# Second half of v for tokens 0 to 255 moved to the third head group, x transpositions, q and k of the next block to later steps

## The chip, the core and the metric

The kernel runs on one core of a Trainium2 chip. Its engines work side by side, each through its own list of instructions: TensorE (PE: matmuls, with weight loads as PEld beside them), VectorE (DVE), ScalarE (ACT), GpSimd (POOL) and SyncE (SP, which issues the DMAs). They wait for each other through semaphores alone. The metric is the device time of one execution in microseconds (us).

## The reference

A transformer block with cross attention, in fp32, for 16 batches of 512 tokens, 512 features and 16 heads of 32, and with a hidden layer of 2048:

```python
q = _layer_norm(query, ln1_g, ln1_b)
qh = (q @ wq + bq).reshape(Bq, Sq, H, hd)
kh = (context @ wk + bk).reshape(Bq, Sc, H, hd)
vh = (context @ wv + bv).reshape(Bq, Sc, H, hd)
scores = jnp.einsum('bqhd,bkhd->bhqk', qh, kh) * scale
allowed = pos_in_block[None, :] <= jnp.arange(Sq)[:, None]
scores = jnp.where(allowed[None, None, :, :], scores, NEG_INF)
probs = jax.nn.softmax(scores, axis=-1)
o = jnp.einsum('bhqk,bkhd->bqhd', probs, vh).reshape(Bq, Sq, Dm)
x = query + o @ wo + bo
h = _layer_norm(x, ln2_g, ln2_b)
return x + jax.nn.gelu(h @ w1 + b1, approximate=False) @ w2 + b2
```

## The kernel before

Two programs follow each other in one launch. Stage A computes attention and writes x to a scratch tensor, stage B the hidden layer. The change touches stage A alone. Every dense product is made of three matmuls, since each fp32 operand is held as a high part and a low part (`_hi`, `_lo`).

Stage A runs over the 16 batches: the first unrolled, batches 1 to 14 in a hardware loop, the last and a tail unrolled. A batch is 48 steps: four head groups (`g` 0 to 3, four heads each) of twelve steps (`k` 0 to 11). Step `k` of a group brings one tile of scores through a pipeline:

- PE forms the scores in `bank_s` (L425). Steps 0 to 3 hold two matmuls (128 and 256 columns), steps 4, 6, 8 and 10 one of 384, steps 5, 7, 9 and 11 one of 512.
- DVE adds the mask and takes the minimum (L574), then moves the transposed probabilities of four steps earlier from `bank_t` to `pT` (L520). For the tiles of steps 5, 9 and 11 ACT makes this move, in its own list at steps 9, 1 and 3.
- ACT takes the exponential (L710).
- PE transposes the tile of three steps earlier into `bank_t` (L437). The tile of step `k-3` needs the bank that the tile of step `k-5` leaves, so PE waits in step `k` for the move made at step `k-1`.

Into each step PE's list puts dense work between the scores and the transpositions. Its place is written out by hand in the table `BESIDE`: for each group the jobs, and how many matmuls of a job stand in which step. The jobs are `Q0` to `Q3` and `K0` to `K3` (q and k of a head group, 12 matmuls of 512 columns; group `g` makes those of group `g+1`, and `Q0`, `K0` those of the next batch), `V0a`, `V0b`, `V1a`, `V1b` (v: 0 and 1 are tokens 0 to 255 and 256 to 511, a and b the two halves of the heads; 24 matmuls of 256 columns, L410), `X0` to `X3` (x of the next batch transposed, L369), `R` (reciprocal sums transposed, L379) and `O0` to `O3` (output product of the batch before). Outside the table, the product with v stands at step 9 for the first pair of query tiles and at step 5 of the next group for the rest (`pv`, L460).

The dense jobs take turns in three banks, `bank_d`, in the order of their first matmuls: a job waits until the job three before it has been read. Who reads is fixed: X by ACT (L676) in the step in which it ends and by DVE (L552) one step later; Q and K by ACT (L686) in the step in which they end and by DVE (L560) one step later; V by ACT (L697); R by ACT (L718). `Q0` waits for DVE's read of the last three X jobs. DVE multiplies by the reciprocals (`o_product`, L584) at step 6. When q and k of a group are split, SP copies them into `stack` with six DMAs of 256 KB (L265), in order; the group's first scores wait for all six. POOL splits the context of the next batch (L773, L775) once `V1b` is done, then expands the reciprocals that the fourth group's `R` needs. SP stores x of `O1` to `O3` and then loads x of the next batch (L336), on which DVE takes statistics at steps 1, 3, 4 and 4 of the third group (L531).

Of the kernel before, what the change touches and what calls it, by code (L numbers as in the profile page):

```python
# [51 lines left out]
def stage_a(nc, x, ctxT, wq, wk, wv, wo, vecs, bo, x1):  # L52
# [21 lines left out]

    BESIDE = [
# [4 lines left out]
    ]  # L80
    TAIL = [("R", {5: 4}), ("O0", {8: 12}), ("O1", {9: 12}), ("O2", {10: 12}), ("O3", {11: 12})]

# [23 lines left out]
    with ExitStack() as ctx:  # L106
# [246 lines left out]
        def _(pe):  # L353
# [86 lines left out]
            def pv(it, g, pair):  # L440

                last_tile = TG * g + (3 if pair == 0 else 11)
                for i in range(2):

                    pe.wait_ge(moved[i], it.b * (TB // 2) + ((last_tile + 1) // 2 + 1))
                if pair == 0:
                    pe.wait_ge(o_prod, it.b * NG + (g + 1))
                if g in (0, 2):

                    name = f"V{pair}{'ab'[g // 2]}"  # L450
                    at = {"V0a": -1, "V1a": 0, "V0b": 1, "V1b": 2}[name]
                    pe.wait_ge(d_free[it.bank(name, at)], it.bank_read(name, at))
                if pair == 0:
                    parts = [(0, 0, 256, 0), (1, 256, 128, 128)]
                else:
                    parts = [(0, 384, 256, 256), (1, 640, 256, 256), (2, 896, 256, 256), (3, 1152, 128, 256)]
                for j, at, w, to in parts:
                    for r in range(4):
                        h = 4 * (g % NG) + r
                        mm = pe.matmul(bank_v[32 * r:32 * r + 32, to:to + w], v_sb[:, j, HD * h:HD * h + HD],  # L460
                                       pT[:, r, at:at + w], start=(j == 0), stop=(j == len(parts) - 1),
                                       skip_group_check=True)
                mm.then_inc(pv_done, 1)
# [24 lines left out]
            def body(it):  # L488
                for n, steps in enumerate(it.steps):
                    g, k = divmod(n, TG)  # L490
                    if not it.tail:
                        score(it, n)
                    for job, i, j in steps:
                        dense_step(it, job, g, i, j)
                    if k == PV1_AT and not (it.first and g == 0):
                        pv(it, g - 1, 1)
                    if k == PV0_AT and not it.tail:
                        pv(it, g, 0)
                    if n >= LAG and not it.tail or n < LAG and not it.first:
                        p_transpose(it, n - LAG)  # L500
# [696 lines left out]
def build(nc, x, ctxT, wq, wk, wv, wo, vecs_a, bo, w1, w2, vecs_b, b2, out):  # L1197
    x1 = nc.dram_tensor("x1_scratch", tuple(x.shape), F32).ap()
    stage_a(nc, x, ctxT, wq, wk, wv, wo, vecs_a, bo, x1)
    stage_b(nc, x1, w1, w2, vecs_b, b2, out)  # L1200
# [41 lines left out]
```

## Time and profile before

| | |
|---|---|
| median of 3 runs | 3095.35 us (3094.23 to 3096.35) |
| the profiled execution | 3096.19 us, span 3094.5 us |
| first scores of stage A | 47.42 us |
| the 14 batches of the loop | 137.7 to 1470.8 us |
| rest of stage A (last batch, tail) | to about 1585 us |
| stage B | the remainder |
| PE busy over the span | 2965.2 us (96%) |
| DVE, ACT, POOL busy | 1520.4, 1153.1, 459.1 us |

Times in views of stretches count from the start of the span. In such a view every engine has its busy time and, in brackets, the number of its instructions; PEclk is the granted clock of TensorE as a share of 2.4 GHz. In the timeline a row holds the start, the duration, the engine, the line and the operation; in square brackets stands how long the engine had been idle before and what released it. PE's rows overlap, because matmuls are pipelined: what a matmul costs is the distance to the start of the next row. The fifth batch of the loop is quoted most: its groups begin at 519.20, 541.33, 568.62 and 591.12 us, and it ends at 614.55 us.

How long a step takes, from the first scores of one step to those of the next (starts of L425 in the timeline), in us; the fourth group is that of batch 7 (781.81 to 803.65 us), where the clock stays at 1.00:

| step | 0 | 1 | 2 | 3 | 4 | 5 | 6 | 7 | 8 | 9 | 10 | 11 |
|---|---|---|---|---|---|---|---|---|---|---|---|---|
| second group | 2.07 | 1.95 | 2.07 | 1.95 | 1.31 | 5.15 | 0.51 | 3.36 | 2.02 | 2.90 | 2.03 | 1.98 |
| third group | 2.06 | 1.95 | 2.06 | 1.95 | 1.30 | 3.79 | 1.93 | 1.00 | 1.86 | 1.94 | 2.08 | 0.56 |
| fourth group | 4.01 | 1.95 | 2.06 | 1.95 | 1.31 | 2.37 | 1.46 | 1.03 | 1.40 | 1.97 | 1.28 | 1.05 |

### The profile page before, as it was taken

The numbers are of one execution on the slowest core, as the hardware profiler recorded it, in microseconds if no ns is written. First come the engines' busy times: TensorE is split into PE (matmuls) and PEld (weight loads), VectorE is DVE, ScalarE is ACT, GpSimd is POOL, SyncE is SP. The second block draws the span as 40 slices with busy tenths as digits, with TensorE's granted clock in tenths as the row PEclk, the third lists the DMA queues.
The fourth block names the chain that finished last, engine by engine and source line by source line (L and its number), as shares of the span: only waits on it lengthen the run. The fifth ranks groups of instructions, "written<-read, shape, count | busy, mean of one in ns | idle before, by whom it ended". The sixth has DMA issues, their size and how long they took to land. (4 is left out here: it accounts for less than half of the span.)

```text
span 3094.5 us, 52560 instructions
## 1 busy us (share of the span) xinstructions
PE 2965.2 (96%) x17576; PEld 2408.6 (78%) x17576; DVE 1520.4 (49%) x4100; ACT 1153.1 (37%) x2958; POOL 459.1 (15%) x432
## 2 busy tenths in 40 slices
PE   6999999999999999999979999999999999999999
PEld 5777877778777777777758888888888888888887
DVE  4766666666676666766634333322333322333322
ACT  3655566555666565655622111111111111111111
POOL 1222122211222112222112000000000000000000
PEclk9999999999999999999979999999999999999999
DMA  5766676666666666666522111100111100111100
GB/s 133 122 113 102 111 107 111 115 110 108 107 108 119 112 102 115 103 119 110 89 85 82 41 41 41 41 9 32 41 41 41 41 31 10 41 41 41 41 27 14
DMA packets 123695, 231.89 MB, mean 75 GB/s; under 512 B 10752, under 2 KB 10752, under 8 KB 123648
## 3 DMA queue, kind: packets, MB, share of 16 engines
q1 hardware_dynamic: 123648, 231.28, 37.5%
q8 instruction: 28, 0.46, 0.1%
q14 instruction: 19, 0.16, 0.0%
HBM read 97.02 MB, written 33.55 MB: 42 GB/s over the span
## 5 line engine op out<-in xcount | busy, mean ns | idle before, releaser
L710 ACT ACTIVATE sm<-sm,mins 128x128 f32<-128x128 f32 (+3 forms) x1024 | 571.7, 559 | 606.4 <-DVE mins L574 603.6
L574 DVE CUSTOM_DVE_ANT_0 sm<-bank_s,mask 128x128 f32<-128x128 f32 (+3 forms) x1024 | 480.7, 488 | 451.2 <-PE bank_s L425 440.5
L1146 ACT ACTIVATE g_sb<-bank_f,b1s 128x512 f32<-128x512 f32 x256 | 176.2, 688 | 1173.1 <-PE bank_f L956 1173.1
L1058 DVE CAST g_hi<-g_sb 128x512 fp32r<-128x512 f32 x256 | 113.0, 441 | 866.9 <-ACT g_sb L1146 866.9
L437 PE MATMUL bank_t<-ident,sm 128*128 128x128 f32 x2560 | 424.1, 281 | 53.5 <-ACT pT L520 34.1
L437 PEld LDWEIGHTS bank_t<-ident,sm 128*128 128x128 f32 x2560 | 305.8, 143 | 156.9 <-issue 76.6
L954 PE MATMUL bank_f<-hT_hi,w_hi 128*128 128x512 f32 x1024 | 407.6, 398 | 1.6 <-DVE hT_lo L1052 1.6
L954 PE MATMUL bank_o<-w_hi,g_hi 128*128 128x512 f32 x1024 | 408.0, 398 | 0.0
L956 PE MATMUL bank_f<-hT_hi,w_lo 128*128 128x512 f32 x1024 | 406.7, 397 | 0.0
L955 PE MATMUL bank_f<-hT_lo,w_hi 128*128 128x512 f32 x1024 | 406.4, 397 | 0.0
L956 PE MATMUL bank_o<-w_hi,g_lo 128*128 128x512 f32 x1024 | 406.3, 397 | 0.0
L955 PE MATMUL bank_o<-w_lo,g_hi 128*128 128x512 f32 x1024 | 405.6, 396 | 0.0
L425 PE MATMUL bank_s<-stack 96*128 96x128 f32 (+3 forms) x1024 | 357.3, 390 | 6.5 <-DMA stack<-st_lo 5.8
L520 DVE COPY pT<-bank_t 128x384 f32<-128x384 f32 (+1 forms) x576 | 326.9, 568 | 0.5 <-PE bank_t L437 0.5
L1190 POOL TENSOR_TENSOR xr<-xr,b_row 128x512 f32<-128x512 f32 x64 | 81.3, 1301 | 1213.2 <-DMA xr<-x_scratch 1213.2
L954 PEld LDWEIGHTS bank_f<-hT_hi,w_hi 128*128 128x128 f32 x1024 | 193.4, 189 | 48.3 <-issue 2.0
L956 PEld LDWEIGHTS bank_f<-hT_hi,w_lo 128*128 128x128 f32 x1024 | 193.7, 189 | 47.4
L955 PEld LDWEIGHTS bank_f<-hT_lo,w_hi 128*128 128x128 f32 x1024 | 193.9, 189 | 46.8
L956 PEld LDWEIGHTS bank_o<-w_hi,g_lo 128*128 128x128 f32 x1024 | 193.1, 189 | 46.6
L955 PEld LDWEIGHTS bank_o<-w_lo,g_hi 128*128 128x128 f32 x1024 | 193.0, 188 | 46.2
L954 PEld LDWEIGHTS bank_o<-w_hi,g_hi 128*128 128x128 f32 x1024 | 192.8, 188 | 45.5
L792 POOL TENSOR_TENSOR oT_lo<-rT,oT_hi 128x512 fp32r<-128x512 f32 x64 | 82.3, 1286 | 814.6 <-ACT oT_hi L724 814.6
(108 smaller groups left out, 4486.5 us busy)
## 6 DMA issues: line engine op xcount, KB each, us to landing
stack<-st_hi SPq DMA_DIRECT2D x256, 256.0 KB, 5.6
xt<-in_x SPq DMA_DIRECT2D x32, 1024.0 KB, 5.3
stack<-st_lo SPq DMA_DIRECT2D x128, 256.0 KB, 7.2
c_raw<-in_ctxT SPq DMA_DIRECT2D x64, 256.0 KB, 6.0
x_scratch<-xt SPq DMA_DIRECT2D x64, 256.0 KB, 2.0
xn<-x_scratch SPq DMA_DIRECT2D x16, 1024.0 KB, 7.7
xr<-x_scratch SPq DMA_DIRECT2D x16, 1024.0 KB, 5.6
out<-xr SPq DMA_DIRECT2D x64, 256.0 KB, 2.1
```

Source lines behind the costliest of these rows:

```text
L425: mm = pe.matmul(bank_s[n % BANKS_S][:, off:off + w], stack[0:96, g % 2, 0, r, P * qt:P * qt + P], stack[0:96, g % 2, 1, r, 0:w], start=Tr ...
L437: mm = pe.transpose(bank_t[n % 2][:, P * c:P * c + P], sm[:, n % SLOTS_S, P * c:P * c + P], ident[:])
L520: copy(out, src).then_inc(moved[n % 2], 1)
L574: op = V.tensor_tensor_reduce(sm[:, n % SLOTS_S, off:off + w], bank_s[n % BANKS_S][:, off:off + w], mask[:, 512 - w:512], 1.0, 0.0, ALU.ad ...
L710: op = A.activation(row, row, ACT.Exp, bias=mins[:, g % 2, c:c + 1], scale=-1.0, accum_out=sums[:, g % 2, c:c + 1])
L792: G_.tensor_tensor(out=oT_lo[:, g % NG, :], in0=rT[:], in1=oT_hi[:, g % NG, :].bitcast(F32), op=ALU.subtract).then_inc(oT_done, 1)
L954: pe.matmul(o, lh, rh, start=first, stop=False)
L955: pe.matmul(o, lh, rl, start=False, stop=False)
L956: return pe.matmul(o, ll, rh, start=False, stop=last)
L1058: V.tensor_copy(g_hi[:, f % RING_H, :], g_sb[:, f % 2, :]).then_inc(g_hi_ok, 1)
L1146: A.activation(g_sb[:, f % 2, :], bank_f[f % 2][:], ACT.Gelu, bias=b1s[:, f:f + 1], scale=1.0).then_inc(gelu, 1)
L1190: G_.tensor_tensor(out=xr[:, t, :], in0=xr[:, t, :], in1=b2_row[:], op=ALU.add).then_inc(xr_ok, 1)
```

## The change

`V0b` leaves steps 10 and 11 of the second group for steps 4 and 5 of the third; `V1b` and the four x transpositions there go one step later; in the fourth group `Q0` goes from steps 0 and 1 to 1 and 2, `K0` from 2 and 3 to 4 and 5, `V0a` from steps 6 to 10 to steps 7 to 11. In `pv` the index under which `V0b` is looked up follows.

```diff
-        [("Q2", ...), ("K2", ...), ("R", {4: 4}), ("O1", {5: 12}), ("O2", {7: 12}), ("O3", {8: 6, 9: 6}), ("V0b", {10: 12, 11: 12})],
-        [..., ("R", {4: 4}), ("V1b", {5: 12, 6: 12}), ("X0", {7: 4}), ("X1", {8: 4}), ("X2", {9: 4}), ("X3", {10: 4})],
+        [("Q2", ...), ("K2", ...), ("R", {4: 4}), ("O1", {5: 12}), ("O2", {7: 12}), ("O3", {8: 6, 9: 6})],
+        [..., ("R", {4: 4}), ("V0b", {4: 12, 5: 12}), ("V1b", {6: 12, 7: 12}), ("X0", {8: 4}), ("X1", {9: 4}), ("X2", {10: 4}), ("X3", {11: 4})],
...
-                    at = {"V0a": -1, "V1a": 0, "V0b": 1, "V1b": 2}[name]
+                    at = {"V0a": -1, "V1a": 0, "V0b": 2, "V1b": 2}[name]
```

The number of instructions of each engine stays as it was. PE's list in the loop, from the third group's step 10 or 11 into the fourth group, right behind the four transpositions of `X3`; before:

```order
L437 MATMUL bank_t1<-ident,sm 128x128 x4
L421 REGISTER_ALU
L425 MATMUL bank_s1<-stack 128x512
L435 REGISTER_ALU
L437 MATMUL bank_t0<-ident,sm 128x128 x3
L420 REGISTER_ALU
L421 REGISTER_ALU
L425 MATMUL bank_s0<-stack 128x128
L425 MATMUL bank_s0<-stack 128x256
L390 REGISTER_ALU
L410 MATMUL bank_d2<-xnT_hi,wq_hi 128x512
```

The same place now:

```order
L435 REGISTER_ALU
L437 MATMUL bank_t0<-ident,sm 128x128 x3
L420 REGISTER_ALU
L421 REGISTER_ALU
L425 MATMUL bank_s0<-stack 128x128
L425 MATMUL bank_s0<-stack 128x256
L437 MATMUL bank_t1<-ident,sm 128x128 x4
L421 REGISTER_ALU
L425 MATMUL bank_s1<-stack 128x128
L425 MATMUL bank_s1<-stack 128x256
L390 REGISTER_ALU
L410 MATMUL bank_d2<-xnT_hi,wq_hi 128x512
```

Between `X3` and the first matmul of `Q0` there stood two sets of transpositions and two of scores; there stand as many now, but both sets of scores are those of the fourth group's steps 0 and 1, and `Q0` has moved behind step 0.

DVE's list in the fourth group in the loop, from K0's low part (`st_lo` with `vec`) to `o_product` (L584) before the change:

```order
L560 SCALAR_TENSOR_TENSOR st_lo<-bank_d,vec,st_hi 128x512
L567 REGISTER_ALU
L574 ISA sm,mins<-bank_s,mask 128x512
L574 ISA mins 128x1
L520 COPY pT<-bank_t 128x384
L567 REGISTER_ALU
L574 ISA sm,mins<-bank_s,mask 128x384
L574 ISA mins 128x1
L520 COPY pT<-bank_t 128x384
L582 REGISTER_ALU
L583 REGISTER_ALU
L584 TENSOR_TENSOR rT<-bank_v,rT 128x512
```

And DVE's step 6 of the same group with what follows it now:

```order
L574 ISA sm,mins<-bank_s,mask 128x384
L574 ISA mins 128x1
L520 COPY pT<-bank_t 128x384
L582 REGISTER_ALU
L583 REGISTER_ALU
L584 TENSOR_TENSOR rT<-bank_v,rT 128x512
L558 REGISTER_ALU
L560 SCALAR_TENSOR_TENSOR st_lo<-bank_d,vec,st_hi 128x512
L567 REGISTER_ALU
L574 ISA sm,mins<-bank_s,mask 128x512
L574 ISA mins 128x1
L520 COPY pT<-bank_t 128x384
```

K0's low part has moved from step 4 to step 6, behind `o_product` and ahead of the mask of step 7.

## Rows read from the trace of the kernel before

**Rows 1.** The page: busy time (share) and instructions

```profile
PE 2965.2 (96%) x17576; PEld 2408.6 (78%) x17576; DVE 1520.4 (49%) x4100; ACT 1153.1 (37%) x2958; POOL 459.1 (15%) x432
```

**Rows 2.** Waits of PE, whole span: total us, times, longest

```profile
PE bank_t L437 <- ACT pT L520: 34.1, 82, 1.4
...
PE bank_d L410 <- DVE xnT_lo L552: 25.6, 15, 1.7
```

**Rows 3.** Stretches: the loop, its batches 6 and 7, third and fourth groups

```profile
137.70:1470.80 1333.10, 1270.45 (x9636) 1038.23 (x9634) 909.00 (x2815) 802.33 (x2297) 293.39 (x295) 0.98 0.65 110
...
614.55:709.90 95.35, 90.89 (x689) 74.28 (x689) 64.90 (x202) 57.36 (x165) 20.98 (x22) 0.98 0.65 110
...
709.90:803.60 93.70, 89.28 (x688) 72.98 (x688) 64.88 (x202) 57.21 (x165) 20.88 (x22) 1.00 0.65 111
...
568.62:591.10 22.48, 20.85 (x175) 17.31 (x174) 18.88 (x59) 15.06 (x45) 5.59 (x7) 1.00 0.65 112
...
781.81:803.65 21.84, 19.77 (x159) 15.73 (x158) 14.77 (x48) 14.16 (x41) 9.11 (x10) 1.00 0.87 165
```

**Rows 4.** Timeline, second group of batch 5, step 10

```profile
564.60 0.42 PE L425 MATMUL bank_s<-stack 96*128 96x384 f32 x1
565.25 0.56 DVE L574 CUSTOM_DVE_ANT_0 sm<-bank_s,mask 128x384 f32<-128x384 f32 x1 [0.94 <-PE bank_s L425]
...
565.74 0.55 DVE L520 COPY pT<-bank_t 128x384 f32<-128x384 f32 x1
...
566.28 0.60 PE L437 MATMUL bank_t<-ident,sm 128*128 128x128 f32 x4
```

**Rows 5.** Timeline of DVE, third group of batch 5, step 1

```profile
572.10 0.64 DVE L531 BATCH_NORM_STATS2 stats<-xt 128x6 f32<-128x512 f32 x1
```

**Rows 6.** Line L336, 560 to 600 us: issue of the x load, its landing

```profile
L336 SPq DMA_DIRECT2D xt<-in_x x1: 405/405/405, 566.5 to 566.5; - x1
...
DMA to landing us min/median/max: 5.2/5.2/5.2
```

**Rows 7.** Timeline, batch 5, from step 10 of the third group to Q0

```profile
589.46 0.56 ACT L520 COPY pT<-bank_t 128x512 f32<-128x512 f32 x1
...
590.17 0.63 PE L437 MATMUL bank_t<-ident,sm 128*128 128x128 f32 x4 [0.84 <-ACT pT L520]
...
592.47 0.68 DVE L552 TENSOR_TENSOR xnT_lo<-bank_d,xnT_hi 128x512 fp32r<-128x512 f32 x1
...
593.30 0.47 PE L410 MATMUL bank_d<-xnT_hi,wq_hi 128*128 128x512 f32 x1 [1.71 <-DVE xnT_lo L552]
```

**Rows 8.** Timeline, batch 5, fourth group, steps 4 to 8

```profile
604.28 0.74 DVE L560 SCALAR_TENSOR_TENSOR st_lo<-bank_d,vec,st_hi 128x512 fp32r<-128x512 f32 x1
...
607.96 0.68 DVE L584 TENSOR_TENSOR rT<-bank_v,rT 128x512 f32<-128x512 f32 x1
...
608.55 0.68 DVE L574 CUSTOM_DVE_ANT_0 sm<-bank_s,mask 128x512 f32<-128x512 f32 x1
...
609.16 0.55 DVE L520 COPY pT<-bank_t 128x384 f32<-128x384 f32 x1
```

**Rows 9.** Timeline of SP, batch 5, the stack copies of Q0 and K0

```profile
599.53 1.21 SPq L265 DMA_DIRECT2D stack<-st_hi  x2
...
605.48 0.56 SPq L265 DMA_DIRECT2D stack<-st_lo  x1
```

**Rows 10.** Tile stack, 591 to 616 us: issue to landing of its six copies

```profile
DMA to landing us min/median/max: 4.2/6.1/8.1
```

**Rows 11.** Stretches: two dips of the clock, and 3.4 us of batches 6 and 7

```profile
594.43:597.84 3.41, 3.41 (x13) 2.82 (x12) 0.81 (x5) 0.67 (x4) 2.62 (x4) 0.51 0.82 290
690.00:693.41 3.41, 3.41 (x13) 2.83 (x12) 0.81 (x5) 0.83 (x4) 2.72 (x4) 0.50 0.77 285
...
686.60:690.00 3.40, 1.69 (x10) 1.29 (x9) 2.92 (x10) 2.07 (x7) 2.31 (x3) 0.99 0.73 177
...
782.10:785.50 3.40, 1.69 (x9) 1.23 (x8) 2.77 (x9) 1.98 (x7) 2.18 (x3) 1.00 0.64 177
```

6 rows, old and new, of the table BESIDE are left out of this document.

## The prediction

> **What bounds the kernel now.** I read the page's first part, then the waits of PE, then stretches of a batch, then the timeline of the places that the change touches. PE is busy 96% of the span [rows 1]; no other engine is near that. What PE loses is in its waits: 34.1 us in 82 short ones for moves by ACT, and 25.6 us in 15 waits of 1.7 us, one a batch, in which `Q0` waits for DVE's low part of `X3` [rows 2]. The 14 loop batches take 1333.1 us, 95.22 each [rows 3]. A batch whose clock stays at 1.00 takes 93.70 us, one with a granted mean of 0.98 takes 95.35 [rows 3], which is 1.6 more: in it TensorE runs for 3.4 us at 0.50 (1.2 instead of 2.4 GHz), right where `Q0` begins after that wait [rows 11]. So a batch costs its PE work, its waits, and a dip. The change takes no instruction away; it can only move time between steps that are full of PE work and steps in which PE waits for the chain scores, mask, move, transpositions.
>
> **The chain, from rows.** From the scores of a step to its mask it is 0.65 us (564.60 to 565.25), from mask to move 0.49 [rows 4]; from the start of a move to the transpositions that wait for it 0.71 (589.46 to 590.17) [rows 7]. So PE's transpositions in step k+1 start no earlier than 1.85 us after the scores of step k (2.15 for the tile of 512), later still where DVE comes late. A step without dense work costs PE itself about 0.55 us, a step with it some 2: a filled step hides the chain, an empty one does not. I carried this forward step by step through one batch, with the durations of rows 4, 7 and 8.
>
> **Second group, steps 10 and 11: -1.9 us.** From 564.60 to the group's end at 568.62 they take 4.02 us; V0b is 1.42 in each (564.60 to 566.28, less 0.26 for the scores) [rows 4]. Without it step 10 takes 0.62, its move having been made in step 9 beside `O3`. Step 11 then waits for the move of step 10: scores 0, mask 0.65, move 1.13, transpositions 1.84, end 2.11. So 2.84 us of work leave, 0.93 come back as waiting.
>
> **What the early third group meets.** `X` for the next batch is loaded by a DMA issued at 566.47 that lands 5.2 us later, at 571.7 [rows 6]; DVE's statistics start at 572.10 [rows 5]. The load hangs on `O3`, which hasn't moved, and DVE now gets there 1.9 us earlier. It therefore stands 1.5 us in step 1, with the masks of steps 2 and 3 behind it. PE has `Q3` and `K3` in these steps; the move that its step 3 needs is made about 0.8 us before it is wanted. I cost this at nothing.
>
> **Third group, steps 4 to 11: +1.3.** Step 4 takes V0b's first half, 1.42, less the short wait for a move that it had before: 2.40 against 1.31 in the table of steps. Steps 5 and 6 hold twelve half-width matmuls as before. Step 7 has `V1b` instead of `X0`, +1.0. The four X steps then take 1.12, 1.94, 1.56 and 1.04 where steps 8 to 11 took 1.86, 1.94, 2.08 and 0.57, since three normalisations on DVE are past by then and step 10's wait for ACT (0.84) [rows 7] shrinks to 0.4. Sum 15.8 against 14.5.
>
> **Fourth group: +1.5.** Without a dip it took 21.84 [rows 3]. `X3` is now followed by four things on DVE before its low part: the moves and masks of steps 11 and 0. Low part to `Q0` is 0.83 us (592.47 to 593.30) [rows 7]. Step 0 is empty and waits 0.8 for its move; `Q0`, now in step 1, waits another 1.5. Together 2.3 against 1.7, and steps 2 to 5, with an empty step 3 and K0 beside R, lose 0.4 more on ACT's move: steps 0 to 5 take 14.2 against 13.7. Then comes a knot. `K0` ends in step 5, so DVE makes its low part (0.74) in step 6 behind `o_product` (0.68) and ahead of the mask of step 7; before, it stood in step 4 [rows 8]. Mask, move, product and low part start to start are 2.2 us, in an empty step and behind a step in which PE has 0.5 us of work. The mask of step 7 starts 2.35 after its scores instead of 0.7, and the transpositions of step 8 wait 1.3 us, where the whole step took 1.40. That is +1.1. Sum 23.4 against 21.84, +1.5.
>
> Without a dip a batch is then 93.7 - 1.9 + 1.3 + 1.5 = 94.7 us (rounded terms; 94.67 by my table).
>
> **Two queues that I cost at nothing.** SP: Q0's and K0's six copies run from an issue at 599.53 to 613.6 (605.48 + 8.1), 14.0 us in order [rows 9, 10], 1.0 ahead of the next batch's first scores at 614.55. Q0's high part is now ready 31.8 us into the third group's time, so the last lands at 45.8, and the batch ends at 47.1. 1.3 us spare. K0's low part comes at 40.9 and is issued in time for that. POOL: contexts wait for `V1b` and shift by 1.1 us; they end near 29.5, the expansion at 30.2, and `R` wants it at 31.7.
>
> **The dips.** Ahead of batch 6's dip (from 686.60) PE is busy for 1.69 us of 3.40, and at the same place of batch 7, which has no dip (from 782.10), it is 1.69 too [rows 11]: what the engine did there doesn't tell the two apart. After the change the place is as empty: from the scores of the third group's step 11 to `Q0` my table has 2.0 us of work in 4.4. So dips don't vanish. But the dips come at 594.43 and 690.00, 95.57 apart [rows 11], while batches are 95.35 long: a batch keeps nearly the same place against them, slides by 0.2, and is missed once in the run. A batch of 94.7 slides by 0.9 when it has no dip, and by 0.7 the other way when it has one (94.7 + 1.6 = 96.3). It should fall in and out of step, about every other batch, with a mean of about 95.57. I take that: 14 x (95.57 - 95.22) = +4.9 us.
>
> By a rule of the Trainium skill ("TensorE: Matmul & The Clock Gate", Why this matters for your kernels) it is long idle gaps between bursts of matmuls that cost the full clock; here dips follow though the longest such gap is 1.71 us [rows 7], in a mix of short waits and transpositions. By the rule, with the longest gap now 1.5, dips would be gone, which is the second rival below.
>
> **Sum.** First batch: +1.2 of steps (its second group has no O jobs, so it gains 1.7), and half of its dip saved, -0.7: +0.5. Loop +4.9. Last batch: no x, `Q0` or `K0`; -1.9 in the second group, +1.3 in the third: -0.6. Stage B unchanged. +4.8 on a span of 3094.5: 3099.3, with the 1.7 around it 3101.0 for the profiled execution's 3096.19. The median of before is 0.8 lower, so 3100.1 in its terms. What a measurement of this kernel can tell is about 0.2%, 6.2 us: that is a tie, 0.16% to the slow side. Own range 3096 to 3105.
>
> **Rivals.**
> 1. The knot and the empty steps are hidden: DVE catches up, no wait over 0.3 at step 8 and X3's low part as before. Against it: rows 8 show DVE without any pause there already. Then 93.7 - 1.9 + 1.3 + 0.4 = 93.5 without a dip, and dips as before (95.1): 14 x -0.2, about 3092 to 3094. Chance 0.1.
> 2. No dips: 14 x (94.7 - 95.22) = -7.3, with the first batch -1.4 and the last: about 3087 to 3089. For it: batch 7 had none with the same work ahead. Against it: the place gets no fuller. Chance 0.07.
> 3. Slower, DVE stands at the x load. Place: third group, step 1. The statistics hold DVE for 1.5 us and the masks of steps 2 and 3 come too late. It decides when the load lands more than 0.8 us after my 571.7 (the wait then gets through to PE's step 3) or when ACT, already behind by the same 1.5, delays the moves of tiles 9 and 11. Price up to 1.5 x 14 = 21 us on top of the sum, 3121; I take half, 3111. Chance 0.13.
> 4. Slower, each batch dips: for it, the emptier stretch; against it, the drift. 14 x (96.3 - 95.22) = +15, and the first batch keeps its dip, +0.7: 3111. Chance 0.15.
> 5. The stack copies land behind the batch's end. For it: only 1.0 us spare before. 2 us late (the last lands 0.7 behind the end) would add 14 x 0.7 = 10 us: 3110. Chance 0.05.
>
> The move cannot fail to happen: PE's list is the table. The forecast has 0.5. It lies at the edge of the tie, so a third of it counts as slower (my table is good to 0.03 a step, 0.4 a batch). Faster 0.12, same 0.5, slower 0.38. Unknown bounds: the price of step 8 is between 0 (DVE hidden) and 2.2 us (the whole of step 6's DVE work), of the load between 0 and 1.5. The range from 3091 to 3111 takes in those cases but rival 2 and the end of rival 3.
>
> **What would show it.** In the profile after: second group 25.4 us without a wait but one of 0.9 in step 11; third group 23.8; `Q0` waiting 1.5 for L552; a wait of 1.3 for DVE's L520 in the fourth group's step 8; 23.4 us for that group where the clock stays; about half the batches at 94.7 and half at 96.3. DVE idle for the x load at L531, some 1.5 x 14 us. I would be wrong if PE waits for `stack`, if R waits for POOL, or if all batches have one length.

## The result, and the profile after

The change takes 3103.83 us (median of 13 runs, 3099.82 to 3106.69) where the kernel before takes 3095.35 (13 runs, 3093.63 to 3101.14): a ratio of 1.0025, 95% interval 1.0016 to 1.0033. It is slower by about 8 us, a little more than the 6.2 us (0.2%) up to which the prediction speaks of a tie. The profiled execution has a span of 3101.7 us.

PE's waits in the profile after (us in total, times, longest), with DVE's for the x load:

```profile
PE bank_t L437 <- DVE pT L520: 45.1, 54, 1.2
...
DVE stats L531 <- DMA xt<-in_x: 24.6, 15, 4.1
PE bank_t L437 <- ACT pT L520: 24.5, 67, 1.6
PE bank_d L410 <- DVE xnT_lo L552: 20.3, 15, 1.4
```

Against [rows 2] the waits for ACT's moves and for `X3` are shorter (24.5 after 34.1, 20.3 after 25.6); the waits for DVE's moves are the costliest now (45.1 after 17.1). The 1.2 of step 8 of the fourth group is among them, once a batch. Stretches like those in [rows 3], after: the loop, batch 5, its second, third and fourth groups, and the dips (3.4 us with a granted clock of 0.50) of batches 5 and 6:

```profile
137.76:1476.21 1338.45, 1266.49 (x9635) 1037.95 (x9634) 904.57 (x2815) 798.76 (x2296) 293.05 (x295) 0.98 0.64 109
520.27:615.88 95.61, 90.47 (x691) 74.14 (x690) 64.61 (x202) 57.05 (x164) 20.94 (x22) 0.98 0.64 110
542.38:567.70 25.32, 24.51 (x171) 19.25 (x170) 15.63 (x48) 12.48 (x39) 0.61 (x1) 1.00 0.60 104
567.70:591.31 23.61, 23.32 (x199) 20.21 (x198) 19.44 (x61) 15.87 (x45) 6.96 (x8) 1.00 0.64 111
591.31:615.88 24.57, 21.14 (x159) 16.90 (x158) 14.84 (x48) 13.88 (x41) 9.06 (x10) 0.93 0.77 149
594.80:598.21 3.41, 3.41 (x11) 2.72 (x12) 0.45 (x3) 1.45 (x5) 2.64 (x4) 0.50 0.77 285
690.37:693.78 3.41, 3.41 (x11) 2.73 (x12) 0.49 (x3) 1.46 (x5) 2.81 (x4) 0.50 0.84 286
```

The loop takes 1338.45 us, 95.60 a batch, after 1333.10 (95.22): 5.35 of the 7.2 us by which the span grew. All 14 batches have a dip now, after 13. Of the rest, 0.4 lies ahead of the first scores, -0.4 in the first batch and 1.7 between the last batch's start and stage B; stage B didn't change (1510.8 both times). The third group came out at 23.61, the second at 25.32, with a wait of 0.64 in step 11:

```profile
567.40 0.55 PE L437 MATMUL bank_t<-ident,sm 128*128 128x128 f32 x3 [0.64 <-DVE pT L520]
```

The wait for `X3` that answers to [rows 7], PE after:

```profile
591.31 0.48 PE L425 MATMUL bank_s<-stack 96*128 96x128 f32 x2
592.47 0.63 PE L437 MATMUL bank_t<-ident,sm 128*128 128x128 f32 x4 [0.68 <-DVE pT L520]
592.85 0.48 PE L425 MATMUL bank_s<-stack 96*128 96x128 f32 x2
594.68 0.66 PE L410 MATMUL bank_d<-xnT_hi,wq_hi 128*128 128x512 f32 x1 [1.35 <-DVE xnT_lo L552]
```

Step 0 (from 591.31) has only its scores and transpositions and waits 0.68, step 1 waits 1.35 for the low part, and Q0's matmuls then run at 0.50 (each 0.43 from the next instead of 0.23). Before there was one wait of 1.71. DVE, whose low part of `X3` ends the wait of step 1, after (L552 twice: `X2`, then `X3`):

```profile
592.24 0.68 DVE L552 TENSOR_TENSOR xnT_lo<-bank_d,xnT_hi 128x512 fp32r<-128x512 f32 x1
...
593.38 0.55 DVE L520 COPY pT<-bank_t 128x384 f32<-128x384 f32 x1
593.85 0.68 DVE L552 TENSOR_TENSOR xnT_lo<-bank_d,xnT_hi 128x512 fp32r<-128x512 f32 x1
```

From 590.37 to 594.45 DVE goes from one instruction to the next without a pause. And the knot that answers to [rows 8], all engines after, steps 6 to 8:

```profile
607.55 0.48 PE L425 MATMUL bank_s<-stack 96*128 96x512 f32 x1
...
607.69 0.56 DVE L574 CUSTOM_DVE_ANT_0 sm<-bank_s,mask 128x384 f32<-128x384 f32 x1 [2.54 <-PE bank_s L425]
...
608.64 0.68 DVE L584 TENSOR_TENSOR rT<-bank_v,rT 128x512 f32<-128x512 f32 x1
...
609.24 0.74 DVE L560 SCALAR_TENSOR_TENSOR st_lo<-bank_d,vec,st_hi 128x512 fp32r<-128x512 f32 x1
...
609.90 0.68 DVE L574 CUSTOM_DVE_ANT_0 sm<-bank_s,mask 128x512 f32<-128x512 f32 x1
...
610.51 0.55 DVE L520 COPY pT<-bank_t 128x384 f32<-128x384 f32 x1
...
611.21 0.63 PE L437 MATMUL bank_t<-ident,sm 128*128 128x128 f32 x4 [1.23 <-DVE pT L520]
```

The scores of step 7 are formed from 607.55, their mask starts at 609.90, 2.35 later; product and low part stand between. DVE had idled 2.54 us right before the mask of step 6.

### The profile page after: what moved, and what is told of

Its sections match the earlier page's. It is cut to its first block and busy times, and to the rows that moved or that the text cites. A ratio compares the mean times of both kernels' runs of the same rounds, so it can differ in the third digit from the quotient of the medians.

```text
span 3101.7 us, 52560 instructions
## 1 busy us (share of the span) xinstructions
PE 2961.6 (95%) x17576; PEld 2407.9 (78%) x17576; DVE 1515.6 (49%) x4100; ACT 1149.3 (37%) x2958; POOL 458.7 (15%) x432
## 5 line engine op out<-in xcount | busy, mean ns | idle before, releaser
L437 PE MATMUL bank_t<-ident,sm 128*128 128x128 f32 x2560 | 423.1, 280 | 69.9 <-DVE pT L520 45.1
```

The costliest lines, as they stand in the source:

```text
L437: mm = pe.transpose(bank_t[n % 2][:, P * c:P * c + P], sm[:, n % SLOTS_S, P * c:P * c + P], ident[:])
```

## The experiments

Each kernel was timed beside the kernel before. "Dips" counts the loop batches with 3.4 us at 0.50, "no dip" is the mean of the loop batches without one, both in the profiled execution. The ratio is that of all executions, and these can have more or fewer dips than the profiled one: those of e3 took 3073.08 to 3084.68 us, and the profiled one is the longest of them; in e9 it is the longest too, in e12 the shortest.

| kernel | no dip, us | dips of 14 | loop mean, us | ratio to before (95%) |
|---|---|---|---|---|
| before | 93.76 | 13 | 95.22 | 1 |
| the change | none | 14 | 95.60 | 1.0025 (1.0016 to 1.0033) |
| e1, third group only | none | 14 | 95.53 | 1.0025 (1.0016 to 1.0034) |
| e2, fourth group only | 93.73 | 2 | 93.95 | 0.9952 (0.9940 to 0.9964) |
| e3, K0 in steps 3, 4 | 93.22 | 8 | 94.03 | 0.9939 (0.9926 to 0.9952) |
| e6, statistics later | none | 14 | 95.56 | 1.0026 (1.0017 to 1.0035) |
| e4, change, wait filled | 94.04 | 0 | 94.04 | 0.9948 (0.9935 to 0.9962) |
| e5, before, wait filled | 93.72 | 0 | 93.72 | 0.9933 (0.9920 to 0.9947) |
| e7, K0 3, 4, V0a from 6 | 93.18 | 7 | 93.88 | 0.9945 (0.9931 to 0.9958) |
| e8, e7, wait filled | 93.23 | 0 | 93.23 | 0.9907 (0.9892 to 0.9922) |
| e9, e7's group, V0b stays | 92.97 | 4 | 93.39 | 0.9913 (0.9899 to 0.9926) |
| e10, V0b's move alone | 93.27 | 9 | 94.29 | 0.9964 (0.9951 to 0.9978) |
| e11, change, x stays | 93.31 | 1 | 93.42 | 0.9918 (0.9904 to 0.9932) |
| e12, e11 with e7's group | 92.47 | 2 | 92.70 | 0.9887 (0.9872 to 0.9902) |

**Which half costs: e1 and e2.** e1, against the change:

```diff
-        [("Q0", {1: 6, 2: 6}), ("R", {4: 4}), ("K0", {4: 6, 5: 6}), ("V0a", {7: 8, 8: 4, 9: 4, 10: 4, 11: 4})],
+        [("Q0", {0: 6, 1: 6}), ("K0", {2: 6, 3: 6}), ("R", {4: 4}), ("V0a", {6: 8, 7: 4, 8: 4, 9: 4, 10: 4})],
```

> The change without its fourth group: V0b, V1b and the x transpositions as in the change, the fourth group as before. Theory A (the steps' waits add up): X3's low part comes one step later, so Q0 in step 0 waits about 3.3 us where it waited 1.7; fourth group without a dip about 23.4 us against 21.84, a loop batch about 94.4 without and 96.0 with a dip, total 0.2 to 0.4% above before. Theory B (the change loses only through its fourth group): a batch of 93.70 - 1.98 + 1.10 = 92.8 without a dip and 94.4 with one, total 0.35% below before.

e2 is the other way about, the change's last row of the table in the kernel before.

> The fourth group of the change alone, the other groups as before. Theory A: X3 is done a step ahead of Q0, so the wait for its low part nearly goes (0.3 us or less), an empty step 0 waits about 0.7 for its move, and the knot at step 8 (1.2 us) stays: fourth group about 21.6 us without a dip, a batch 93.4; with dips in all batches 95.0 (0.1% below before), with none 0.8% below. Theory B: the fourth group costs its 1.15 us whatever stands ahead, a batch of 94.85 without and 96.4 with a dip, 0.5% above before.

e1 is as slow as the change. Its longest wait for `X3` is 2.9 us, its batch 95.53 with a dip in each; theory A had 96.0 and 3.3, theory B 94.4. B is out. e2 is 0.48% faster than before, without any move of v. Its batch without a dip is 93.73, hardly off the 93.76 of before, but only 2 of 14 have a dip: A expected 93.4 and left the dips open. So the fourth group's table alone comes out even in the time of its steps: steps 0 to 5 take 12.99 us after 13.65, since the wait of 1.71 for `X3` has gone and one of 1.11 for a move has come, and steps 6 to 11 take 8.83 after 8.20, by the knot. It takes `Q0` out of the wait, and with it most dips.

**Are the dips made there: e4 and e5.** Matmuls whose result nobody reads are added ahead of `Q0`'s wait for the x jobs, six in the change (e4) and seven in the kernel before (e5):

```diff
+                        if it is not pro:
+                            for _ in range(6):
+                                pe.matmul(bank[:], w_hi[0][:, 0, 0:P], w_hi[0][:, 0, :], start=True, stop=True)
                         for m in range(QT - BANKS_D, QT):
```

> The change with six matmuls of 512 columns of no use (wq_hi by wq_hi, into the bank that Q0 will clear) in PE's list ahead of Q0's wait for X3. Theory A (the half clock follows from how little PE does around that wait, and costs 1.57 us a batch): no dips in the 14 loop batches, each 94.0 us instead of 95.60, total 22 us below the change (0.5% below before), and Q0's first matmul no later. Rival (the dips come at their times whatever PE does, or the wait is then longer by the added 1.3 us): batches of 95.6 or more, total as the change or up to 18 us above it.

> The kernel before with seven such matmuls ahead of Q0's wait. Theory A: no dips in the loop, every batch 93.7 us, total 20 us below before (0.65%). Rival: as before or above it.

e4, PE at the place of the wait, and batch 5 and the loop as stretches:

```profile
589.31 0.48 PE L428 MATMUL bank_s<-stack 96*128 96x128 f32 x2
589.62 1.56 PE L390 MATMUL bank_d<-wq_hi 128*128 128x512 f32 x6
591.14 0.47 PE L413 MATMUL bank_d<-xnT_hi,wq_hi 128*128 128x512 f32 x1
```

```profile
140.48:1457.10 1316.62, 1263.68 (x9720) 1034.94 (x9718) 904.69 (x2815) 798.93 (x2296) 293.41 (x295) 1.00 0.65 111
516.74:610.77 94.03, 90.25 (x697) 73.90 (x695) 64.61 (x202) 57.07 (x164) 20.98 (x22) 1.00 0.66 112
```

`Q0` starts 1.83 us after the scores of step 1, as in the change (592.85 to 594.68), the six matmuls fill the wait, the clock stays at 1.00, and a batch takes 94.04 instead of 95.60: a dip costs 1.56 us. In e5 no batch has one either, the kernel before gains 0.67%, and its batch of 93.72 is that of before without a dip (93.76): the seven added matmuls cost nothing. The rival, dips at their times whatever PE does, is out. e4 also gives what the profile of the change doesn't show, its batch without a dip: 94.04, 0.28 above before (second group -1.98, third +1.12, fourth +1.14). So the loop's 5.35 us are 14 x 0.28 = 3.9 for the steps and 1.6 for one dip more.

**The knot: e3 and e7.** e3, against the change, and e7, against e3:

```diff
-        [("Q0", {1: 6, 2: 6}), ("R", {4: 4}), ("K0", {4: 6, 5: 6}), ("V0a", {7: 8, ...
+        [("Q0", {1: 6, 2: 6}), ("K0", {3: 6, 4: 6}), ("R", {4: 4}), ("V0a", {7: 8, ...
```

```diff
-        ... ("V0a", {7: 8, 8: 4, 9: 4, 10: 4, 11: 4})],
+        ... ("V0a", {6: 8, 7: 4, 8: 4, 9: 4, 10: 4})],
```

> The change with K0 in steps 3 and 4 instead of 4 and 5. Theory A (the knot of K0's low part and the product in DVE's step 6 makes the wait at step 8): the wait of 1.2 us in step 8 shrinks to about 0.6, the group is 0.6 to 0.7 us shorter (22.3 without a dip), a batch 93.4 without and 95.0 with a dip, total about 9 us below the change. Rival (step 8 waits because the steps 6 and 7 ahead of it are empty or short, whatever DVE has to do): the wait stays above 1 us and the total within 3 us of the change.

> The change with K0 in steps 3 and 4 and V0a in steps 6 to 10 as before. Theory A: no empty step 6 and no knot; steps 5 to 11 as before the change (10.55 us), fourth group 22.2 without a dip, a batch 93.3 without and 94.9 with a dip, total 0.15% below before. Rival (the loss sits in steps 0 to 2, behind X3): within 3 us of the change.

e3, PE and DVE from step 7's scores:

```profile
603.52 0.47 PE L425 MATMUL bank_s<-stack 96*128 96x512 f32 x1
...
604.61 0.68 DVE L584 TENSOR_TENSOR rT<-bank_v,rT 128x512 f32<-128x512 f32 x1
...
605.21 0.68 DVE L574 CUSTOM_DVE_ANT_0 sm<-bank_s,mask 128x512 f32<-128x512 f32 x1
...
606.51 0.63 PE L437 MATMUL bank_t<-ident,sm 128*128 128x128 f32 x4 [0.57 <-DVE pT L520]
```

With the low part gone from step 6 the wait is 0.57 instead of 1.23, as expected, though the steps 6 and 7 on PE are as short as in the change. The fourth group is 22.2 us against 23.0, a batch 93.22. The total gained more than expected, 0.86% against the change, because 6 of 14 batches of the profiled execution have no dip any more. e7 adds nothing to e3 that can be told: steps 6 to 8 take 1.45, 1.04 and 1.39 where e3 has 0.51, 1.53 and 1.84, and both sum to 3.88. The last step takes 1.2 in both (without a dip) instead of 1.04; in e7 PE waits there for the stack in 6 batches. I had expected a fourth group of 22.2; it is 22.1. The total, 0.55% below before, went past the 0.15% expected by the dips alone.

In e3 and e7 dips come in about every other batch, though both are the change itself up to the end of `Q0`, with the same waits of 0.68 and 1.35. So it isn't the place ahead of `Q0` alone that decides. e7, batches 5 and 6 of the loop, then the dip of batch 5 and the next one, in batch 7:

```profile
513.30:607.88 94.58, 90.69 (x689) 74.30 (x689) 64.51 (x202) 57.41 (x164) 20.73 (x22) 0.98 0.66 111
607.88:701.12 93.24, 89.13 (x689) 73.04 (x689) 64.94 (x202) 57.53 (x165) 21.21 (x22) 1.00 0.66 112
```

```profile
588.54:591.95 3.41, 3.41 (x12) 2.83 (x11) 0.72 (x5) 1.12 (x6) 2.13 (x3) 0.50 0.63 245
776.27:779.68 3.41, 3.41 (x12) 2.77 (x11) 0.59 (x5) 1.15 (x5) 2.34 (x3) 0.50 0.64 247
```

A batch with a dip and one without take 187.82 us together, and the two dips are 187.73 apart, as are all the dips of e7.

**The x load: e6.**

```diff
-    STATS_AT, NORMALISE_AT = (1, 3, 4, 4), (5, 6, 6, 7)
+    STATS_AT, NORMALISE_AT = (2, 3, 4, 4), (5, 6, 6, 7)
```

> The change with the first x statistics in step 2 of the third group instead of step 1, so that DVE need not stand at the x load. Theory A (that stand is hidden): DVE's wait for the load at L531 falls from 24.6 us to under 6 in total, PE's steps stay as they are, total within 0.1% of the change. Rival (the load is what costs): 0.5 to 1.5 us less a batch, total 7 to 20 us below the change.

DVE's waits for the load, e6:

```profile
DVE stats L531 <- DMA xt<-in_x: 3.8, 1, 3.8
```

Of 24.6 us 20.8 are gone, and the time hasn't moved (1.0026 after 1.0025). What DVE stood waiting for the load was fully hidden.

**Both cures together: e8** (e7 with e4's six matmuls).

> The kernel with K0 in steps 3 and 4 and V0a in steps 6 to 10, and six matmuls of no use ahead of Q0's wait. If both theories A hold, their gains add: batches of 93.3 without a dip, total 0.8 to 0.9% below before, the fastest of all. If not, no better than the better of the two alone.

0.93% below before: they add. Its 14 batches, none with a dip, take 93.23 each, as e7's without one do (93.18).

**What moves alone: e9 to e12.** e9 has the kernel before with `Q0` in steps 1 and 2, `K0` in 3 and 4, `V0a` from 6. e11 is one edit against the change; e10 has it and the fourth group of before, e12 and the fourth group of e7:

```diff
-        ... ("X0", {8: 4}), ("X1", {9: 4}), ("X2", {10: 4}), ("X3", {11: 4})],
+        ... ("X0", {7: 4}), ("X1", {8: 4}), ("X2", {9: 4}), ("X3", {10: 4})],
```

> The kernel before with the fourth group Q0 in steps 1 and 2, K0 in 3 and 4, V0a in 6 to 10; V0b and x stay. Theory (Q0's wait for X3, not the fourth group's own table, brings the half clock, and K0 in steps 3 and 4 unties the knot): fourth group 20.8 us, a batch 92.7 with few or no dips, total 1.1% below before. Rival (the fourth group's gains don't add without V0b moved): no better than the run with the change's fourth group alone, 0.5% below.

> V0b and V1b in the third group as in the change, x transpositions in steps 7 to 10 and the fourth group as before. Theory (the move of V0b gains by itself 0.8 us a batch, and the later x takes it back): Q0 waits 1.7 us or less as before, a batch 92.9 without and 94.5 with a dip, total about 0.35% below before. Rival (filling the third group costs what the second saves): a batch of 93.7 to 94.0 without a dip, total as before.

> The change with the x transpositions left in steps 7 to 10. Theory (it is X3's place right ahead of Q0 that costs): no wait for X3's low part, next to no dips, a batch 92.9, total about 1% below before, 1.2% below the change, by one column of the table. Rival (the x transpositions would only wait for DVE in steps 7 to 10 beside V1b, and the time stays in the third group): batches of 93.8 or more, total 0.3% below before or less.

> V0b and V1b as in the change, x in steps 7 to 10, Q0 in steps 1 and 2, K0 in 3 and 4, V0a in 6 to 10. If the gains add: a batch 91.9, no dips, total about 1.5% below before, the fastest. Rival: the stack copies of K0, which land at the batch's end already, set a floor; then PE waits for the stack in every batch and the batch stays above 92.5.

e10: the move of V0b gains 0.36% by itself. Its second group is 25.31 after 27.29, its third 24.04 after 22.50, so 0.44 a batch in these two (0.49 in all) and not the 0.8 expected: steps 9 and 10 of the third group take 2.05 and 1.86 where the change has 1.93 and 1.54, the wait for ACT's move in step 10 being 0.62 instead of 0.30. The rest of its gain is five batches without a dip, after one. The 0.35% expected was met by a smaller gain in the steps and fewer dips. e11, PE at the start of the fourth group, and the loop:

```profile
583.71 0.47 PE L425 MATMUL bank_s<-stack 96*128 96x128 f32 x2
585.29 0.63 PE L437 MATMUL bank_t<-ident,sm 128*128 128x128 f32 x4 [1.11 <-DVE pT L520]
585.68 0.48 PE L425 MATMUL bank_s<-stack 96*128 96x128 f32 x2
585.99 0.40 PE L410 MATMUL bank_d<-xnT_hi,wq_hi 128*128 128x512 f32 x1
```

```profile
137.32:1445.24 1307.92, 1244.24 (x9636) 1021.20 (x9634) 906.58 (x2815) 800.88 (x2296) 294.03 (x295) 1.00 0.66 112
```

No wait for `X3`, one of 1.11 in its place, then `Q0` at full clock: 1 dip in 14. e10 has batches as long (93.27 for 93.31) with the wait of 1.71 ahead of `Q0`, and 9 dips: at the same length the place decides. The batch without a dip is 93.31 where 92.9 was expected, as the third group is e10's 24.05. So the x transpositions one step later, which make the third group 0.43 shorter (24.04 to 23.61), make the fourth 1.16 longer (21.83 to 22.99) and bring 13 dips back. They alone turn a kernel 0.82% faster than before into one 0.25% slower.

e9 and e12 gained less than expected (92.97 for 92.7, 92.47 for 91.9). Between them lies the move of V0b, and it is worth 0.50 a batch here too. PE's waits for the stack, e12, and the stretch of its loop:

```profile
PE bank_s L425 <- DMA stack<-st_lo: 9.6, 13, 5.9
```

```profile
138.42:1436.18 1297.76, 1248.90 (x9633) 1023.75 (x9633) 908.03 (x2813) 805.09 (x2296) 293.07 (x295) 1.00 0.66 113
```

The waits for the stack were 5.8 us in two; here they are 13, of which 12 stand at the end of loop batches, 0.24 on average. The last step takes 1.21 instead of 1.04 (1.29 in e9), so the stack costs some 0.2 a batch; the larger part of e12's miss is again the third group, 24.05. The rival of the floor is half right. e12 is the fastest of all, 3060.05 us, 1.13% below before.

## Why the prediction was right, and where not

The time was in the range, on the slow side of the tie: 3100.1 forecast, 3103.8 measured, +4.8 us against about +8. The three chances don't follow from the list above them: rivals 3 to 5 have 0.33 together, and with a third of the forecast's 0.5 slower comes to 0.50 and not 0.38, which makes it the likeliest outcome.

**Second group, -1.9.** Right: 25.31 against 27.29, step 11 waits 0.64.

**Third group, +1.3.** 23.61 against 22.50, +1.1. Steps 4 to 11 take 15.6 where 15.8 was forecast.

**Fourth group, +1.5.** The mechanism was right at each place (0.68, 1.35 and 1.23 where 0.8, 1.5 and 1.3 stood), the sum too large: 22.99 in e4 and +1.15 where 23.4 and +1.5 stood. Steps 0 to 5 take 14.16 for 14.2, and step 8 has grown by 1.10 (1.40 to 2.50) as forecast. The term that was too large is the rest, steps 6 to 11: 23.4 less 14.2 leaves 9.2 for them, and they take 8.83. The +1.1 of step 8 was charged in full, but together these steps grew by 0.63 only (from 8.20). V0a's four matmuls that left steps 6 and 7 took 0.45 with them, and in step 11, where they stand now, they cost nothing: it takes 1.04 after 1.05. One thing is missing from the chain to `X3`'s low part: DVE does five things ahead of it and not four, `X2`'s low part (592.24) being the fifth; the wait came out at 1.35 all the same.

**So a batch without a dip was mis-sized**: 94.7 forecast, 94.04 measured, that is +0.28 and not +0.9 against before.

**The dips, about every other batch.** Wrong for the change: all 14 have one. With the measured size my own reasoning gives that: 94.04 + 1.56 is 95.60, next to the 95.57 from one dip to the next (594.80 to 690.37), so a batch hardly slides and has one each time. The mean of 95.57 a batch held (95.60) because too long a batch and too few dips cancelled. That was luck, not insight. Rival 4 (each batch dips) was right on the count, and its batch of 96.3 too long by the same 0.7. The drift itself shows in e3 and e7: same place ahead of `Q0`, shorter batch, 8 and 7 dips instead of 14. It shows in the kernel before, too: its 13 dips begin 74.05 to 75.47 us into their batches, and in the batch without one the place 95.57 behind the last dip lies at 75.64 (785.54), later than in any other. So the two stretches of [rows 11] are not quite at the same place: the second lies some 0.15 us later in its batch. That this decides was argued from such distances; no run shifted the batches against the dips and left everything else alone.

**Costs set at nothing.** The x load: shown by e6; DVE stood 1.47 us at it, as worked out:

```profile
572.74 0.69 DVE L531 BATCH_NORM_STATS2 stats<-xt 128x6 f32<-128x512 f32 x1 [1.47 <-DMA xt<-in_x]
```

SP: no wait for the stack at the end of a batch in the change, but e7, e9 and e12 meet that floor as the batch gets shorter. POOL: `R` never waits for it.

**No dips (rival 2).** It didn't happen: the longest gap fell from 1.71 to 1.35 and there was one dip more. The dips go when the place is filled (e4), and nearly so when `Q0` follows an empty step without a second wait (e11, 1 in 14). The rule of the Trainium skill beside it ("TensorE: Matmul & The Clock Gate", Why this matters for your kernels: long idle gaps between bursts), taken for the only cause, would have had no dips in either kernel; the trace disagrees, with 13 and 14.

**First batch and last.** +0.5 and -0.6 forecast, -0.4 and +1.7 measured. The first batch had a dip (from 116.53 us) and has none now, where the forecast counted half of it. In the last batch the second group gave 1.9 and the third took 1.5, near the forecast; the 2.2 left are behind them. There TensorE stands at half clock for 10.24 us (from 1550.53) after 6.83, and step 5 of the fourth group takes 4.40 after 2.37. That batch has no `Q0` or `K0` beside its steps; what decides the length of this stay wasn't tested.

## What to carry to other kernels

Two things pay for an edit to a hand-written order: the steps' own waits, and the clock that a lull leaves behind. Here a wait of 1.7 us cost 1.56 more in the matmuls after it, and taking these dips away by filling it (e5, 0.67%) was worth more than moving V0b alone (e10, 0.36%). Before moving work into a step, list what its result releases: `X3` one step later made its group 0.43 us shorter and the next 1.16 longer. Count the dips of a profile, too, before you read a small difference as work saved: one dip is 1.56 us, and a batch 0.8 us shorter had 8 of them for 14. And where a wait can't be moved, matmuls of no use in it can pay, as long as they end before the wait does.

## What the runs showed of the hardware that I had not expected

- Six matmuls into a bank that will be cleared, in a wait of 1.35 us, left the start of `Q0` where it was and gave back 1.56 us a batch (e4).
- Of two batches with the same busy time of PE ahead, one had a dip and one not [rows 11]; an empty step with one wait of 1.11 us before `Q0` brought 1 dip in 14 (e11), two waits of 0.68 and 1.35 brought 14 (the change), and 8 and 7 in the shorter batches of e3 and e7.
- The kernel before with the change's fourth group (e2) has batches of the same length without a dip (93.73 and 93.76) and yet is 0.48% faster, with 2 dips for 13.
